# Groups of 8, 16, 24, 12 and 4 tiles, rings of eight quads, first norms shared with ScalarE, ranks in other places

## The reference

```
g = graph_layer(layernorm(x), adj)
graph_layer(h):    n = layernorm(h)*gamma+beta;  h + relu((adj @ n) @ W_rel + b_rel + n @ W_root)
x = x + g
x = x + moe(layernorm(x))
moe(z):            scores = z @ Wg.T + bg;  top 2 of 8 experts, softmax over the two
                   sum over the two: p_e * (relu(z @ W1[e].T + b1[e]) @ W2[e].T + b2[e])      hidden width 512
```

## Time and profile before

| | us |
|---|---|
| median of 3 runs | 490.55 (486.5 to 491.15) |
| the profiled execution's own time | 491.38 |
| its span, first to last instruction | 489.6 |
| PE busy | 395.2 (81%) |
| DVE busy | 323.0 (66%) |
| ACT busy | 263.0 (54%) |
| POOL busy | 250.1 (51%) |
| mean granted TensorE clock | 0.927 |

### The profile page before, as it was taken

One profiled execution on the slowest core, in us unless ns is written; L12 is line 12 of the kernel. 1 busy time (PEld: TensorE's weight loads), 2 busy tenths in 40 slices (PEclk: granted clock), 3 DMA queues, 4 the chain that ended last, 5 costly groups with the idle time before them and its releaser, 6 DMA issues.

```text
span 489.6 us, 13203 instructions
## 1 busy us (share of the span) xinstructions
PE 395.2 (81%) x4371; PEld 351.5 (72%) x4371; DVE 323.0 (66%) x1079; ACT 263.0 (54%) x548; POOL 250.1 (51%) x263
## 2 busy tenths in 40 slices
PE   2878697659999779889868999899999999999000
PEld 1773554549998678888757988789999999998000
DVE  4967764873869876666869557575468554588511
ACT  1556636336886747776624786345565555555000
POOL 3001730277700177775007777777777740677770
PEclk9988969998999999999979999999999999999655
DMA  8990741143433444534326456556868867655520
GB/s 275 390 413 37 270 91 22 44 108 104 119 72 56 93 98 115 145 92 112 54 66 161 126 110 125 109 130 143 174 136 175 202 150 109 137 153 141 167 75 32
DMA packets 100721, 65.30 MB, mean 133 GB/s; under 512 B 66866, under 2 KB 92466, under 8 KB 100020
## 3 DMA queue, kind: packets, MB, share of 16 engines
q1 hardware_dynamic: 66292, 34.68, 28.1%
q0 software_dynamic: 8192, 16.79, 12.8%
q10 hardware_dynamic: 26176, 12.98, 10.8%
HBM read 19.58 MB, written 31.85 MB: 105 GB/s over the span
## 4 chain that ended last, share of the span: by engine, by line
PE 57%; DVE 24%; issue 6%; ACT 6%; POOL 3%; DMA 2%; ACTq 0%; DVEq 0%; SPq 0%; POOLq 0%
PE PY L930 7%; PE PY L935 7%; PE PY L931 7%; PE PH L911 7%; PE PH L913 7%; PE PH L912 7%; DVE HL L510 5%; POOL YG L296 3%; PE PY L922 2%; DVE STI L350 2%; PE PA L840 2%; PE PA L841 2%; DVE STO L396 2%; PE PB L832 1%; PE PC L847 1%
## 5 line engine op out<-in xcount | busy, mean ns | idle before, releaser
L283 POOL DMA_INDIRECT rows<-XHL,IDX x128 | 124.6, 973 | 136.3 <-DVE IDX L492 98.2
L510 DVE SCALAR_TENSOR_TENSOR HL<-PH,HH 128x512 f16<-128x512 f32 x198 | 129.9, 687 | 70.8 <-ACT HH L718 68.7
L296 POOL DMA_INDIRECT YG<-yrows,IDX x128 | 121.3, 947 | 91.3 <-DMA yrows<-YB 53.2
L718 ACT ACTIVATE HH<-PH 128x512 f16<-128x512 f32 x198 | 115.5, 594 | 44.7 <-PE PH L913 39.5
L930 PE MATMUL PY<-W2H,HH 128*128 x792 | 132.3, 221 | 0.0
L931 PE MATMUL PY<-W2H,HL 128*128 x792 | 132.3, 221 | 0.0
L911 PE MATMUL PH<-XT,W1H 128*128 128x256 f16 x396 | 110.2, 278 | 3.5 <-issue 1.5
L913 PE MATMUL PH<-XT,W1L 128*128 128x256 f16 x396 | 110.2, 278 | 0.0
L912 PE MATMUL PH<-XT,W1H 128*128 128x256 f16 x396 | 110.1, 278 | 0.0
L935 PE MATMUL PY<-W2L,HH 128*128 x792 | 109.8, 221 | 0.0
L726 ACT ACTIVATE YB<-PY 128x256 f32<-128x256 f32 x99 | 38.0, 384 | 93.5 <-PE PY L935 86.5
(11 more groups left out here) (186 smaller groups left out, 505.7 us busy)
## 6 DMA issues: line engine op xcount, KB each, us to landing
yrows<-YB ACTq DMA_DIRECT2D x47, 256.0 KB
rows<-XT SPq DMA_DIRECT2D x2, 3072.0 KB, 16.4
YG<-in_w SPq DMA_DIRECT2D x2, 2048.0 KB, 11.3
out<-X SPq DMA_DIRECT2D x16, 256.0 KB
X<-in_x SPq DMA_DIRECT2D x3, 1024.0 KB, 5.3
ADJ<-in_adj SPq DMA_DIRECT2D x32, 64.0 KB
rows<-XHL,IDX POOLq DMA_INDIRECT x128, 2.6
YG<-yrows,IDX POOLq DMA_INDIRECT x128, 2.5
```

The costliest lines, as they stand in the source:

```text
L283: nc.gpsimd.indirect_dma_start(rows[g % 2], bass.IndirectOffsetOnAxis(ap=IDX[:, col:col + 1], axis=0), XHL[:, src:src + 2 * P].bitcast(F32 ...
L296: nc.gpsimd.indirect_dma_start(YG[g % 2][:, dst:dst + P], None, yrows[g], bass.IndirectOffsetOnAxis(ap=IDX[:, col:col + 1], axis=0)).then_ ...
L510: nc.vector.scalar_tensor_tensor(HL[:, at:at + 2 * BW], PH[p % 2 * 2 + h][:, :], 0.0, HH[:, at:at + 2 * BW], ALU.max, ALU.subtract).then_i ...
L718: nc.scalar.activation(HH[:, at:at + 2 * BW], PH[p % 2 * 2 + h][:, :], ACT.Relu).then_inc((hia_made, hib_made)[h], 1)
```

## The change

- Groups are 8, 16, 24, 12 and 4 tiles: quads 0-1, 2-5, 6-11, 12-14, 15, with 15, 23, 31, 19 and 11 blocks, again 99. Groups 2, 3 and 4 begin at blocks 38, 69 and 88 (before 38, 61 and 84).
- `XHL` and `YG` become rings of eight quads (`RQ`, `RT`) of the same size as before. `split_high(n)` waits, from quad 8 on, for the whole scatter of the group that quad n - 8 is in; `gather` waits quad by quad for the combine of quad n - 8. The DRAM buffers for rows have 31 and 23 blocks instead of 24 and 24, and the fills with zeros that go with them; the table of constants is 64 columns longer.
- Ahead of block 0 ScalarE makes the norms, in and out, of quads 1, 3 and 5 (`h0_make`, `norm_out`), VectorE those of 0, 2 and 4; there is one semaphore for each of the two engines. ScalarE's list is reordered around them.
- Quads 4 and 5 are scored ahead of the weight pieces 12 to 15, which use bank PA in place of PC; `rank(1)` stands between the products of these pieces.
- In the loop `rank(g)` follows `hidden`; `route_blocks(1)` moves from block 1 to 5; the four tables are new.

```diff
-GS = (8, 16, 16, 16, 8)
+GS = (8, 16, 24, 12, 4)
 G = len(GS)
...
+RQ = 8
+RT = RQ * GT
...
-START = {6: 4, 7: 6, 8: 8, 9: 10, 10: 17, 11: 20, 12: 23, 13: 26, 14: 39, 15: 43}
-STATS = {2: 1, 3: 12, 4: 35}
-ROUTE = {2: 16, 3: 32, 4: 49}
-COMBINE = {0: 30, 1: 32, 2: 66, 3: 68, 4: 70, 5: 72, 6: 90, 7: 92, 8: 94, 9: 96}
+START = {6: 5, 7: 7, 8: 9, 9: 11, 10: 13, 11: 15, 12: 24, 13: 27, 14: 30, 15: 42}
+STATS = {2: 1, 3: 18, 4: 36}
+ROUTE = {2: 21, 3: 36, 4: 48}
+COMBINE = {0: 30, 1: 32, 2: 66, 3: 68, 4: 70, 5: 72, 6: 86, 7: 88, 8: 90, 9: 92, 10: 94, 11: 96}
...
         ADJ = sb("ADJ", [P, 4 * GW])
-        YG = [sb("YG0", [P, 2 * TM * P]), sb("YG1", [P, 2 * TM * P])]
+        YG = sb("YG", [P, 2 * RT * P])
+        W1F, W2F = YG[:, 0:E * HID], YG[:, E * HID:2 * E * HID]
         W1H = sb("W1H", [P, E * HID], F16)
...
         RAO, RTO = sb("RAO", [P, 2 * GT]), sb("RTO", [P, 2 * GT])
-        XHL = sb("XHL", [P, 2 * TM * 2 * P], F16)
+        XHL = sb("XHL", [P, RT * 2 * P], F16)
         LG = sb("LG", [P, TILES * E])
...
         PA, PB, PC = pb("PA"), pb("PB"), pb("PC")
-        WB = PA, PB, PH[0], PH[1], PH[2], PC, PY, PH[3]
+        WB = 2 * [PA, PB, PH[0], PH[1]] + [PH[2], PC, PY, PH[3]] + [PH[2], PA, PY, PH[3]]
...
+        def by_dve(n):
+            return n < Q0[2] and n % 2 == 0
+        def wait_normalized(engine, n, dve_sem, act_sem):
+            if by_dve(n):
+                engine.wait_ge(dve_sem, n // 2 + 1)
+            else:
+                engine.wait_ge(act_sem, n + 1 - len([k for k in range(n) if by_dve(k)]))
         def hi_lo(n):
-            g = group_of(n, Q0)
-            t = g % 2 * TM + (n - Q0[g]) * GT
+            t = n % RQ * GT
             v = XHL[:, t * 2 * P:(t + GT) * 2 * P].rearrange("p (t s d) -> p s t d", s=2, d=P)
...
                 sp.wait_ge(zero_made, 1)
-                sp.dma_start(rows[b].rearrange("(p n b) d -> p n (b d)", p=P, n=4),
-                             ZERO.unsqueeze(1).to_broadcast([P, 4, ZW])).then_inc(zero_out[b], 16)
+                sp.dma_start(rows[b].rearrange("(p b) d -> p (b d)", p=P).rearrange("p (n w) -> p n w", n=4),
+                             ZERO[:, 0:ZW[b]].unsqueeze(1).to_broadcast([P, 4, ZW[b]])).then_inc(zero_out[b], 16)
...
                         col = 2 * T0[g] + k * GS[g] + t
-                        src = (g % 2 * TM + t) * 2 * P
+                        src = (T0[g] + t) % RT * 2 * P
                         nc.gpsimd.indirect_dma_start(
...
                     pool.wait_ge(y_out[j], 16 * turns(C0[g + 1], j, YR))
-                if g >= 2:
-                    pool.wait_ge(combined, Q0[g - 1])
                 for t in range(GS[g]):
+                    n = Q0[g] + t // GT
+                    if t % GT == 0 and n >= RQ:
+                        pool.wait_ge(combined, n - RQ + 1)
                     for k in range(2):
                         col = 2 * T0[g] + k * GS[g] + t
-                        dst = (t * 2 + k) * P
+                        dst = ((T0[g] + t) % RT * 2 + k) * P
                         nc.gpsimd.indirect_dma_start(
-                            YG[g % 2][:, dst:dst + P], None, yrows[g],
-                            bass.IndirectOffsetOnAxis(ap=IDX[:, col:col + 1], axis=0)).then_inc(gathered[Q0[g] + t // GT], 16)
+                            YG[:, dst:dst + P], None, yrows[g],
+                            bass.IndirectOffsetOnAxis(ap=IDX[:, col:col + 1], axis=0)).then_inc(gathered[n], 16)
...
                         t = n * GT + k
-                        y = tile(YG[g % 2], (t - T0[g]) * 2 + e)
+                        y = tile(YG, t % RT * 2 + e)
                         pr = 2 * T0[g] + e * GS[g] + t - T0[g]
...
             norm_in(0)
-            norm_in(1)
             for i in range(4):
...
             norm_in(2)
-            norm_in(3)
...
                 norm_out(n)
-                norm_out(n + 1)
...
             norm_in(4)
-            norm_in(5)
             route_slots(0)
...
                     route_rows(1)
-                if p == 1:
+                if p == 5:
                     route_blocks(1)
...
                 act.wait_ge(stats_made, g + 1)
-                act.wait_ge(xnT_done, n - 3)
-                act.wait_ge(xlo_made, n - 3)
+                act.wait_ge(ones_made, 1)
+                if n >= 4:
+                    act.wait_ge(xnT_done, n - 3)
+                    act.wait_ge(xlo_made, n - 3)
                 for k in range(GT):
...
                 act.wait_ge(stats_made, g + 1)
-                act.wait_ge(h0_made, n + 1)
+                wait_normalized(act, n, h0_dve, h0_act)
                 for k in range(GT):
...
             def split_high(n):
-                act.wait_ge(xn_made, n + 1)
-                g = group_of(n, Q0)
-                if g >= 2:
-                    act.wait_ge(scattered[g - 2], 2 * GS[g - 2] * 16)
+                wait_normalized(act, n, xn_dve, xn_act)
+                if n >= RQ:
+                    g = group_of(n - RQ, Q0)
+                    act.wait_ge(scattered[g], 2 * GS[g] * 16)
                 nc.scalar.activation(hi_lo(n)[0], quad(N4, n).rearrange("p (t d) -> p t d", d=P), ACT.Copy,
...
+            h0_make(1)
             for n in (0, 1):
...
                 u_copy(n)
-            for n in (0, 1):
-                plus_norm(n)
+            plus_norm(0)
+            h0_make(3)
+            plus_norm(1)
             for n in (2, 3):
...
                 u_copy(n)
-            for n in (2, 3):
-                plus_norm(n)
+            plus_norm(2)
+            norm_out(1)
             for n in (0, 1):
...
                 xnT_copy(n)
+            plus_norm(3)
+            h0_make(5)
             four_high(0)
...
                 u_copy(n)
-            for n in (4, 5):
-                plus_norm(n)
+            norm_out(3)
             for n in (2, 3):
...
                 xnT_copy(n)
-            for c in (8, 12):
-                four_high(c)
-                four_low(c)
+            for n in (4, 5):
+                plus_norm(n)
+            four_high(8)
+            four_low(8)
+            norm_out(5)
             for n in (4, 5):
...
                 xnT_copy(n)
+            four_high(12)
+            four_low(12)
             act.wait_ge(b2_made, 2)
...
             pe.wait_ge(score_made, 4)
-            for c in (8, 12):
-                four_whole(c)
-                four_rest(c)
+            four_whole(8)
+            four_rest(8)
             for n in (4, 5):
...
                 score(n)
-            pe.wait_ge(wlo_made, 16)
+            pe.wait_ge(score_made, Q0[2] - 1)
+            four_whole(12)
+            rank(1)
+            four_rest(12)
...
                     pe.wait_ge(experts_made, P0.index(p) + 1)
+                e = expert(p)
+                if p == 1:
+                    pe.wait_ge(wlo_made, 16)
+                hidden(p, e)
                 for g, at in ROUTE.items():
...
                         rank(g)
-                e = expert(p)
-                hidden(p, e)
-                if p == 0:
-                    rank(1)
                 for n, at in START.items():
...
```

More of the change, by code:

```diff
@@ L45 @@
 NEG = -3.0e38
-K_ID, K_ONE, K_M, K_E, K_BREL, K_BG, K_DESC, K_FIRST, K_GAM, K_BET, K_END = (
-    0, 128, 256, 384, 512, 640, 648, 656, 656 + NBM, 657 + NBM, 658 + NBM)
+K_ID, K_ONE = 0, P
+K_M = K_ONE + E * TM
+K_E, K_BREL, K_BG, K_DESC, K_FIRST = K_M + P, K_M + 2 * P, K_M + 3 * P, K_M + 3 * P + E, K_M + 3 * P + 2 * E
+K_GAM, K_BET, K_END = K_FIRST + NBM, K_FIRST + NBM + 1, K_FIRST + NBM + 2
 H_ID, H_NEG, H_NEG2, H_TRI, H_ONE, H_B2M, H_END = 0, 128, 256, 384, 512, 640, 768
-START = {6: 4, 7: 6, 8: 8, 9: 10, 10: 17, 11: 20, 12: 23, 13: 26, 14: 39, 15: 43}
-STATS = {2: 1, 3: 12, 4: 35}
-ROUTE = {2: 16, 3: 32, 4: 49}
-COMBINE = {0: 30, 1: 32, 2: 66, 3: 68, 4: 70, 5: 72, 6: 90, 7: 92, 8: 94, 9: 96}
+START = {6: 5, 7: 7, 8: 9, 9: 11, 10: 13, 11: 15, 12: 24, 13: 27, 14: 30, 15: 42}
+STATS = {2: 1, 3: 18, 4: 36}
+ROUTE = {2: 21, 3: 36, 4: 48}
+COMBINE = {0: 30, 1: 32, 2: 66, 3: 68, 4: 70, 5: 72, 6: 86, 7: 88, 8: 90, 9: 92, 10: 94, 11: 96}
 def turns(n, j, ring):
@@ L77, in sem @@
             return ctx.enter_context(nc.semaphore(name))
-        rows = [nc.dram_tensor(f"rows{b}", [BW * (NBM + 1), P], F32, kind="Internal").ap() for b in range(2)]
+        rows = [nc.dram_tensor(f"rows{b}", [BW * max(NB[b::2]), P], F32, kind="Internal").ap() for b in range(2)]
         yrows = [nc.dram_tensor(f"yrows{g}", [BW * NB[g], P], F32, kind="Internal").ap() for g in range(G)]
@@ L130, in build @@
         B2F, BT = HL[:, :].bitcast(F32), HH[:, 0:E * P]
-        ZW = 2 * (NBM + 1) * P // 4
-        ZERO = XT[:, 0:2 * ZW].bitcast(F32)
+        ZW = [2 * max(NB[b::2]) * P // 4 for b in range(2)]
+        ZERO = XT[:, 0:2 * max(ZW)].bitcast(F32)
         PH = [pb(f"PH{k}") for k in range(4)]
@@ L157, in build @@
         stats_made, sum_made = sem("stats_made"), sem("sum_made")
```

(27 more changed lines are left out.)

12 lines of the change are left out of this document (6 added, 6 removed).

## The result

The kernel after took 492.94 us (median of 10 runs, 492.24 to 494.94), the kernel before 490.21 (10 runs): a ratio of 1.0066, with an interval of 1.0043 to 1.0088. That is slower by 2.7 us, where 490.0 was forecast. The profiled execution of after has a span of 491.5 and its own time was 493.3, near its median.

What follows compares the result with a forecast made beforehand. It took GpSimd's gathers to bound the end and TensorE's pace blocks 53 to 98. Front gains spent on group 2's scatter left block 53 +0.5, the tail -1.3: span 488.8, time taken as 490, range 482 to 498.

Steps and rivals of the forecast that it cites:

- Before block 0: Ahead of block 0, shared norms and reordered scores bring output(0) at 86.9 instead of 89.90, 3.0 us earlier.
- Blocks 0 to 5: Quad 6 a block later, route_blocks(1) moved: 4.3 us won in all, bounds 2 and 7; quad 6's transposes near 107.1.
- the upper bound of 4.5: Gain in us ahead of block 0 if the drop of the clock there goes too; the lower bound is 0.
- Up to the ninth weight piece: Ahead of block 0, the shared norms bring 1.3 us by the ninth weight product.
- From quad 6's transposes to the slots: Stretch of six dense quads up to group 2's slots: 93.4 us, where before it took 73.4.
- rival (d): Slower: group 2's 48 scatters in a row take more than 1.28 us each; at 1.4 us, 496; chance 0.04.
- The wait in block 35: ScalarE stands about 15 us at split_high(14) until group 2's whole scatter lands at 263.3; bounds 9 and 19.
- T to block 41: From T, the end of group 2's scatter at 263.3, to block 41's copy: 27 us, bounds 25 and 30.
- blocks 41 to 53: 12 blocks at 2.75 us, quad 15 5.7, rank(4) 1.0: 39.7 us, before 46.6; block 53 at 330.0.
- the tail: At the end, 80 gathers in one queue, the last at 476.5 against 477.31: 1.3 us earlier relative to the blocks.
- Rival (a): Slower: six dense quads cost 6.2 us each instead of 5.1, group 2's scatter ends 6.5 later: 496.5; chance 0.15.
- Rival (b): Faster: group 2's mask and slots cost TensorE nothing and blocks 0 to 5 win 7 us: 484; chance 0.17.

Runs made afterwards that it cites:

- the front alone: The kernel after with the groups and tables of before, ranks ahead of hidden and route_blocks(1) at block 1: 487.54 us, ratio 0.9949.
- With the clock held: The kernel after with spare TensorE products, 5 + 5 + 3 around quads 4 and 5's transposes, 17 ahead of output(4): 489.45 us, ratio 0.9979.
- the kernel with the ranks alone: The kernel before with one edit, rank(2), rank(3) and rank(4) behind hidden instead of ahead of it: 480.68 us, ratio 0.9789.
- half of the scatters left out: The kernel after with 24 scatter DMAs of group 2 instead of 48, all waits on them lowered to match: 481.89 us, ratio 0.9844.
- the last kernel: The kernel after with rank(2), rank(3) and rank(4) ahead of hidden again, as before: 502.48 us, ratio 1.0244.

## Why the prediction was wrong

**Where it failed.** The two front terms. "Before block 0" was to win 3.0 and won 1.1 (output(0) at 88.77, not 86.9; on the old groups the front alone won 2.1 to 2.7 in time); "Blocks 0 to 5" was to put quad 6's transposes at 107.1 and they came at 110.2. All that stands behind them is late by some 3 us: the scatter of group 2 started at 204.2 (200.5) and its wait ended at 266.2 (263.3), block 53 came at 333.6 (330.0), the span is 491.5 (488.8). I had booked the drop of the clock only as something to be won besides (the upper bound of 4.5), and drew the lower bound from a table and a wait; that the new order could itself run at half clock was in no term. It put the scores of quads 4 and 5 and four weight pieces behind three waits in a row, and output(4) behind one of 4.20. With the clock held there, block 0 is 1.9 earlier than in after, the transposes 3.2, the scatter 3.5, block 53 2.8 and the time 3.5. That half clock at these places costs the missing 3.5 us is shown. That the new front has more of it than the old one is not: it moves from execution to execution, and the kernel with the ranks alone, whose front is the old one, had it over 12.8 us from the ninth weight piece to output(0), nearly the 13.7 of after.

**Luck in the term.** Up to the ninth weight piece 1.3 was forecast and 3.7 came; from there to output(0) 1.7 was to be won and 2.5 was lost. With the clock held it was 2.9 (63.66 for 66.53) and 0.2 (23.2 us for 23.4), so even there the sum of 3.0 came out of two wrong halves, and the reordering was worth next to nothing. How much the sharing of norms is worth stays open: the ninth piece starts at 62.2 to 63.8 in the eleven kernels with the new front, at 66.5 and 65.0 in the two with the old one. Among the other kernels that share the front, groups and ranks of after, the scatter is 2.7 to 4.7 late in all, but where it is lost differs: with half of the scatters left out quad 6's transposes came at 107.95, only 0.9 late, and the dense stretch behind took 1.3 longer than forecast.

**What held.** From quad 6's transposes to the slots 93.4 was forecast and 93.5 came (110.21 to the cast at 203.72; 93.2 to 94.8 in the five other kernels with these groups and ranks behind hidden), with the ring, the ranks and six dense quads in it; two dense blocks and a quad took 10.64 us (10.6). The 48 scatters ran at 1.27 against 1.28; rival (d), the slower pitch, did not come. The wait in block 35 was there, released by that scatter: 11.27 us against 15 (bounds 9 and 19). It is shorter because block 23's copy came at 204.47, not near 198 (for which the prediction gives no working), and block 34's with it at 254.53 (248); that costs nothing, since the end of the wait is the scatter's. TensorE idled 9.6 (10), at half clock after it. T to block 41 took 27.6 (27), blocks 41 to 53 39.8 (39.7). The gathers of groups 2 to 4 ran as one list, and the tail gave back 2.3 (1.3).

**Rival (a)** had the sign that came, by another cause: the dense stretch did hold its 5.1 us a quad. Rival (b) named the ranks behind hidden. Of their 9.5 us in after (the last kernel) 3.3 lie ahead of the scatter, where the sum has 1.3; the rest lies behind it, where (b) did not look.

**What the sum hid.** It ran the edits through one chain and never priced them apart. Apart, the ranks are worth 9 us; in the sum stand 1.3 for rank(2) and 3.7 for rank(4) (4.7 less 1.0), and nothing for rank(3). The groups with their places cost 14.3. Its total came close because large parts of opposite sign, each mis-sized, nearly cancel; whoever had chosen among the parts by its terms would have kept the one that costs most. Of the 14.3, the halved scatter shows 11.0 in the time (492.9 to 481.9), 9.9 of it behind block 34. The rest fits the 4.33 us of idle time in block 38 less what the tail gives back, but that pile was not taken away in any run, so this part is argued.

**The clock.** The Trainium skill ("TensorE: Matmul & The Clock Gate", section "What's actually happening") has idleness take the array to 1.2 GHz until activity releases it. The rows agree: 1.92 against 1.02 us for a pair of weight products, 0.42 against 0.28 for a block's products. I cited it for the wait in block 35, where the clock turned out to be worth nothing (38 spare products, 492.73), and not for the front, where it was worth 3.5.

## What to carry to other kernels

Before you reorder TensorE's work, list its waits in the new order and leave room in the sum for half clock behind them: here ten microseconds of products behind waits of 1.2, 1.3 and 0.9 us ran at half clock. Compare a term of a microsecond with more than one execution: the front of one and the same code differed by 1.5 us. A cross-engine product (here a rank that waits for a mask) belongs behind work that is ready. When a long list of DMAs releases a buffer or a load, its end is the date that counts: ask what must be in front of it and behind it in the queue, and run each edit alone before adding them up.

## What the runs showed of the hardware

A shorter idle time of TensorE can be worth more than itself, but its length alone does not tell: with 3.57 instead of 4.88 us ahead of rank(3) one kernel kept the full clock behind it (0.28 us for the next product) and another did not (0.39), and moving three such ranks brought about 9 us in both (in the second with route_blocks(1) moved too). Thirteen and seventeen spare products, which compute nothing that is used, brought 3.5 us (492.94 to 489.45), while 38 at another place brought nothing measurable. Indirect DMAs issued by GpSimd kept a mean pitch of 1.25 to 1.28 us in every kernel, 0.95 busy and 0.30 between them, beside busy engines as in the idle tail.
